# Cross attention: the copy of the third turned tile is put ahead of the additions of head 1's output products on VectorE

## The reference

```
Q = input_Q @ Wq.T + bq ; K = ctx @ Wk.T + bk ; V = ctx @ Wv.T + bv      (16 heads x 64)
scores  = Q K^T / sqrt(64)
attn    = softmax(scores, axis=-1)
context = attn @ V ; out = context @ Wo
x = layernorm(x + out)
```

## Time and profile before

| what | value |
|---|---|
| time, median of 3 runs | 1234.19 us (1233.22 to 1238.19) |
| the profiled execution's own time | 1238.3 us |
| its span, first to last instruction | 1236.6 us |
| mean granted TensorE clock | 0.963 of full speed |
| busy TensorE, weight loads | 1090.7 us (88%), 725.3 us (59%) |
| busy VectorE, ScalarE, GpSimd | 743.3 us (60%), 707.9 us (57%), 174.6 us (14%) |
| cross attention, group 0 | from about 197 us to 311 us; a pair takes 12.5 us |

### The profile page before, as it was taken

One profiled execution on the slowest core, in us unless ns is written; L12 is line 12 of the kernel. 1 busy time (PEld: TensorE's weight loads), 2 busy tenths in 40 slices (PEclk: granted clock), 3 DMA queues, 4 the chain that ended last, 5 costly groups with the idle time before them and its releaser, 6 DMA issues.

```text
span 1236.6 us, 23850 instructions
## 1 busy us (share of the span) xinstructions
PE 1090.7 (88%) x8477; PEld 725.3 (59%) x8477; DVE 743.3 (60%) x2028; ACT 707.9 (57%) x1913; POOL 174.6 (14%) x290
## 2 busy tenths in 40 slices
PE   3789999997889998999698999899879999899967
PEld 2564685554766487555486458555557638755546
DVE  5542575888644265788754338578874416667761
ACT  3361586775555076777465238677645607777724
POOL 4320120013120021002301012000322002200000
PEclk9799999999899999999799999999979999999968
DMA  7400000000000000000000000000000000000000
GB/s 230 122 1 1 1 0 2 2 27 1 1 11 1 0 1 1 1 28 1 2 1 11 1 1 0 1 2 27 2 1 9 1 1 1 0 1 2 2 1 9
DMA packets 21061, 15.59 MB, mean 13 GB/s; under 512 B 871, under 2 KB 18644, under 8 KB 20956
## 3 DMA queue, kind: packets, MB, share of 16 engines
q1 hardware_dynamic: 20956, 14.24, 3.9%
HBM read 13.18 MB, written 1.05 MB: 12 GB/s over the span
## 4 chain that ended last, share of the span: by engine, by line
PE 51%; issue 30%; DVE 9%; ACT 4%; POOL 3%; POOLq 1%; SPq 1%; DVEq 1%; DMA 0%; ACTq 0%
PE ps L716 9%; PE ps L870 4%; PE ps L789 4%; PE ps L901 4%; PE ps L886 4%; DVE nmax L1909 3%; PE ps L754 3%; PE ps L748 3%; PE ps L809 2%; PE ps L797 2%; PE ps L745 2%; PE ps L910 2%; POOL rstd L1448 2%; DVE X L1918 1%; PE ps L617 1%
## 5 line engine op out<-in xcount | busy, mean ns | idle before, releaser
L1086 ACT ACTIVATE arena<-ps 128x256 f32<-128x256 f32 (+2 forms) x336 | 176.3, 534 | 118.4 <-PE ps L886 46.4
L1280 ACT ACTIVATE arena<-ps,nmax 128x512 f32<-128x512 f32 x256 | 174.2, 684 | 40.3 <-DVE nmax L1909 40.0
L1909 DVE TENSOR_REDUCE nmax<-ps 128x1 f32<-128x512 f32 x256 | 161.1, 683 | 20.0 <-PE ps L870 20.0
L886 PEld LDWEIGHTS ps<-ident,arena 64*128 64x128 f32 x2048 | 79.4, 139 | 83.9 <-ACT arena L1280 55.5
L1914 DVE COPY arena<-ps 128x512 f32<-128x512 f32 x128 | 87.9, 687 | 63.0 <-PE ps L886 62.4
L716 PE MATMUL ps<-big,w1a 128*128 128x512 f32 x256 | 117.3, 604 | 0.0
L886 PE MATMUL ps<-ident,arena 64*128 64x64 f32 x2048 | 93.1, 227 | 17.3 <-DVE arena L1914 10.5
L1446 POOL TENSOR_TENSOR vare<-mv,eps_ln 128x2 f32<-128x2 f32 x64 | 13.3, 208 | 593.5 <-DVE mv L1576 593.2
L1249 ACT ACTIVATE arena<-ps,snm 128x136 f32<-128x136 f32 x256 | 91.7, 374 | 5.6 <-DVE snm L1839 5.6
L1918 DVE SCALAR_TENSOR_TENSOR X<-ps,rinv,X 128x128 f32<-128x128 f32 x256 | 72.5, 344 | 13.2 <-PE ps L910 12.0
L716 PEld LDWEIGHTS ps<-big,w1a 128*128 128x128 f32 x256 | 46.3, 189 | 57.5 <-issue 56.5
(11 more groups left out here) (349 smaller groups left out, 2126.1 us busy)
## 6 DMA issues: line engine op xcount, KB each, us to landing
ctx<-in_ctx_dram SPq DMA_DIRECT2D x4, 512.0 KB, 4.1
w1a<-in_L_ffn_W_dram SPq DMA_DIRECT2D x1, 2048.0 KB, 9.5
w1b<-in_L_ffn_W_dram SPq DMA_DIRECT2D x1, 2048.0 KB, 12.1
w2b<-in_L_ffn_W_dram SPq DMA_DIRECT2D x8, 256.0 KB, 6.8
X<-in_x_dram SPq DMA_DIRECT2D x4, 256.0 KB, 2.9
out_dram<-Y SPq DMA_DIRECT2D x4, 256.0 KB, 2.5
arena<-in_L_xattn_Wq_dram SPq DMA_DIRECT2D x1, 512.0 KB
arena<-in_L_xattn_Wk_dram SPq DMA_DIRECT2D x1, 512.0 KB
```

The lines of the kernel that those rows point to most:

```text
L886: last = pe.transpose(ps[:, 4 + u, o:o + DK], cprob[r, 2 * (t % 2) + h, k * P:(k + 1) * P], ident[r, r])
L1086: return act.activation(dst, src, ACT.Copy)
L1280: act.activation(cprob[:, 2 * (t % 2) + h, :], bank(2 * (t % 2) + h), ACT.Exp, bias=nmax[:, s:s + 1], accum_out=rsum[:, j % 2, s:s + 1]).t ...
L1909: dve.tensor_reduce(nmax[:, s:s + 1], bank(s % 4), AX.X, ALU.max, negate=True)\
```

## The change

On VectorE, in each pair of cross attention, the four additions of head 1's products are done after the copy of the third turned tile (tile 2) and no longer before it. They now stand between that copy and the two row maxima that follow it. Two drains are added: one ahead of that copy, one at the end of the pair ahead of the wait and the reciprocal. TensorE, ScalarE, GpSimd and the transfers are untouched.

```
--- before.py
+++ after.py
@@ -1941,10 +1941,12 @@
                     for t in range(QT):
                         for h in range(2):
                             row_max_ahead(j, t, h)
-                    if j:
-                        add_head(j - 1, 1)
                     for t in range(QT, TT):
+                        if t == 2:
+                            dve.drain()
                         turned(j, t)
+                        if t == 2 and j:
+                            add_head(j - 1, 1)
                         for h in range(2):
                             row_max_ahead(j, t, h)
                         if t == 2 and j == PAIRS - 4 and more_groups:
```

## The result

The changed kernel takes 1244.19 us (median of 8 runs, 1240.6 to 1248.2) against 1237.64 us for the kernel before (8 runs, 1233.22 to 1238.58). The ratio is 1.0064, 95% interval 1.0049 to 1.0079: slower, by between 0.5% and 0.8%. The profiled execution took 1242.75 us, its span is 1241.0.

The account below looks back on a forecast made before the run. TensorE was taken to bound the kernel (51% of the chain), with a VectorE detour in ordinary pairs. 9.45 + 1.32 + 0.45 + 0.84 + 4.0 - 3.22 - 0.28 - 1.61 = +10.95 on 1234.19 gave 1245.1 us, range 1237.5 to 1252.

Parts of the forecast that it names:

- the clock: Pairs 6 and 7, three groups: half clock behind four of six long TensorE waits, 1.0 us each, +4.0 us.
- the drains: End of pairs 6 and 7 of three groups: six exposed drains at 0.14 us each, +0.84 us.
- Ordinary pairs: Pairs 1 to 3 of three groups, 1 to 5 of the last: 14 gains of 0.23 us, 3.22 in sum.
- Pair 4: Pair 4 of three groups: VectorE is short and idles until tile 2 arrives, 0.44 us lost each, 1.32 in sum.
- Last group, pair 6: No query projection covers ScalarE's copy of tile 3, so the value products wait for it: 0.45 us lost.
- pair 7: Last group: no row maxima follow and the turning ends earlier, -0.28 us.
- The nine releases: Pairs 5, 6 and 7 of groups 0 to 2: TensorE's bank 7 waits end 1.05 us later each, +9.45 us.
- The last group's fall: Last group: TensorE's 1.42 us wait shrinks to about 0.8, under 1.19, so its half-clock stretch goes, -1.6 us.
- the clock holds: Rival: no half clock in pairs 6 and 7, the last group's stays; +8.6 us, 1242.7 us, chance 0.28.

Follow-up runs that it names:

- short filler: Changed kernel plus one unread 512-column matmul into bank 0 ahead of TensorE's bank 7 wait, pairs 6 and 7, groups 0 to 2: ratio 1.0058.
- drains-only kernel: Kernel before with the two new drains added and the additions left where they were: ratio 1.0004.
- that kernel with the TensorE move: Kernel before with TensorE's three bank 7 consumers in pairs 5, 6 and 7 put behind the turning of tile 3: ratio 0.9999.
- the kernel put together: Changed kernel with additions moved only in chosen pairs, two projections behind tile 3's turning, no drain ahead of tile 2: 1226.55 us, 0.9927 to the kernel before.

## Why the prediction was right, point by point

The time, 1244.19, is 0.9 from the forecast sum of 1245.1, and the sign and the mechanism held. The shift is a fairer measure, because the median of before came out at 1237.64 with more runs: forecast +10.95, measured +6.6 by the medians and +7.9 by the ratio. Term by term the sum fits better than that. Without the clock and the drains it had +7.7 for cross attention, and the kernel with the short filler, which has no falls in pairs 6 and 7, measures +7.4 (393.1 less 385.7). What the sum lacks is a term for the untouched code between the groups' cross attentions: it is 3.0 and 4.0 us shorter in the two traces of the changed kernel than in the kernel before.

- Ordinary pairs: 0.23 each, 14 times. Measured 12.50 to 12.27, with the early half of the turning, the exponential as releaser and the late row maxima as described. Shown also by moving them alone.
- Pair 4: 0.44 forecast, 0.45 measured. Last group, pair 6: 0.45 and 0.46; pair 7: -0.28 and -0.31.
- The nine releases: 1.05 each forecast. Measured 0.98 in pair 5, 1.04 in pair 6 and 1.03 in pair 7 (short filler), 9.15 in sum for 9.45. The idle stretches of pairs 6 and 7 are 1.82 us as forecast, and TensorE's wait in pair 5 is 0.91 for 0.98. When TensorE asks later, the waits are gone, so the cause is shown. The prediction counted nine waits in all; the view behind the earlier trace rows also lists three weight loads of L901, for head 0's additions, but they are 3.0 us before and after, so the sum is not touched.
- The drains, +0.84: this term was wrong in its place. It stood at the end of pairs 6 and 7, where the drains-only kernel shows nothing. The price of an exposed drain is 0.17 to 0.19, not 0.14, but the place where it would be exposed (between additions and copy) no longer exists in the changed order.
- The clock, +4.0: the falls came, four or five of six, and five cost 4.8 us in cross attention (397.9 less 393.1), the four of the second trace 3.7. What the sum missed is that the rest of the program does not stay as it was: in traces with falls the half-clock stretch behind the layer norm is mostly shorter. Keeping the clock up all through pairs 6 and 7 moved the ratio only from 1.0064 to 1.0058. By the two intervals the net worth of the falls can be zero and is hardly above 3.5 us.
- The last group's fall, -1.6: it was indeed gone in both traces after, and the tail is 2.0 and 2.6 us shorter. TensorE's idle stretch there did shrink, from 1.42 to 0.83 us, as forecast:

```profile
1188.06 0.99 PE L886 MATMUL ps<-ident,arena 64*128 64x64 f32 x16 [0.83 <-DVE arena L1914]
```

The reason given, that the stretch is then under 1.19, is not shown by it, because a longer one did no harm either. In the drains-only kernel the same stretch is 1.60 us long. Its row in that kernel's timeline:

```profile
1182.63 0.72 PE L886 MATMUL ps<-ident,arena 64*128 64x64 f32 x16 [1.60 <-DVE arena L1914]
```

No fall followed, as the same kernel's busy times by stretch say (granted clock 1.00):

```profile
1183.00:1187.00 4.00, 3.20 (x42) 2.33 (x39) 2.85 (x10) 0.98 (x2) 0.20 (x1) 1.00 0.01 4
```

The rival "the clock holds" (1242.7, +8.6) described the time as well as the forecast did, though not the trace. Against the measured +7.9 it is the nearer sum, since what the clock took in cross attention and gave back elsewhere nearly cancelled. That the absolute forecast hit is partly luck: a sum 3 us too high stood on a median 3.5 us too low.

What stays open: why the drains-only kernel's 4.0 us in cross attention do not show in its time, and how the rest of the program's clock depends on where cross attention ends. The stretches outside cross attention, which no experiment touched, differ by up to 7.2 us between the traces (1236.6 - 385.7 - 202.5 = 648.4 in the kernel before; 1246.5 - 402.9 - 201.9 = 641.7 with the change in pairs 5 to 7 only; 1244.9 - 394.7 - 201.3 = 648.9 without the drain ahead of tile 2). So a difference of 2 or 3 us between two whole kernels is explained here only as far as it lies in the pairs or in the tail.

## What to carry to other kernels

When work is moved behind another step on one engine, list every wait for the moved work's count, in every special case of the loop: here 14 plain iterations gained 0.23 us each and 9 special ones lost 1.0 (three more, where VectorE is short, lost 0.45), and one look at who waited for the additions named the nine. The remedy was not to undo the move but to let the waiting engine ask one step later as well, and to choose the order pair by pair: 0.7% faster than before (some three quarters of it in the changed pairs), where the plain move was 0.6% slower. A gain on one engine's wait is capped by the next releaser of the same instruction, so read both of them before pricing it.

## What the runs showed of the hardware that was not expected

- TensorE's falls to half clock (1.2 GHz) repeat for one kernel in part. The two traces of the kernel before have all ten half-clock stretches at the same places to 0.1 us; those of the changed kernel share four falls and differ in the fifth. The places do not follow from the length of an idle stretch alone. Within 2 us behind one of 1.42 or 1.43 us came a fall in 4 of 9 cases (both traces of the kernel before, one of four in that kernel with the TensorE move, one of three in the kernel put together). Behind 1.60 us in the last pair there was none in two kernels (drains only, and the change in pairs 5 to 7 only). Behind 1.82 us there was one in 15 of 24 (five, four, five and, without the drain ahead of tile 2, one of six).
- A fall in or just behind pair 7 went with a shorter half-clock stretch at the following layer norm: 10.2 us in 8 of 9 cases over all traces, against 13.7 us in 25 of the 30 cases without. That is an association read from traces, not a cause shown.
- A VectorE drain on the chain costs 0.17 to 0.19 us, and nothing where the engine waits behind it.
